# Two column halves: splitting every convolution matmul of an ODE-net kernel into two 64-column matmuls

## The reference

```
def _L0_conv_ref(x):                       # a DCT over rows and columns
    y = jnp.einsum('kh,bchw->bckw', Dh, x)
    y = jnp.einsum('lw,bckw->bckl', Dw, y)
    return y

def odefunc(t, y):                         # the second layer
    h = jax.nn.relu(_group_norm(y, gn1_w, gn1_b))
    h = _concat_conv(t, h, conv1_w, conv1_b)      # 3 x 3, 33 -> 32 channels, one of them is t
    h = jax.nn.relu(_group_norm(h, gn2_w, gn2_b))
    h = _concat_conv(t, h, conv2_w, conv2_b)
    return _group_norm(h, gn3_w, gn3_b)

def step(y, t):
    return (y + dt * odefunc(t, y), None)  # NUM_STEPS = 6, dt = 1/6
```

## Time and profile before

| what | us |
|---|---|
| median of 2 runs (3930.53 to 3938.78) | 3934.66 |
| span of the profiled execution | 3928.6 |
| PE busy (91% of the span) | 3592.0 |
| PEld busy (52%) | 2039.1 |
| DVE busy (85%) | 3342.3 |
| ACT busy (53%) | 2079.6 |
| POOL busy (24%) | 929.9 |

### The profile page before, as it was taken

How to read it: one execution, slowest core, us unless ns; L and a number is a source line. 1 busy time by engine, 2 the same in 40 slices (tenths; PEclk the granted TensorE clock), 3 DMA queues, 4 the chain that set the end, 5 groups by cost and what they waited for, 6 DMA issues and landing times.

```text
span 3928.6 us, 70526 instructions
## 1 busy us (share of the span) xinstructions
PE 3592.0 (91%) x21844; PEld 2039.1 (52%) x21844; DVE 3342.3 (85%) x7423; ACT 2079.6 (53%) x3169; POOL 929.9 (24%) x1589
## 2 busy tenths in 40 slices
PE   3699999999999999999999999999999999999995
PEld 3455554555555555555555555555555555554553
DVE  7688888888888888888888888888888888888885
ACT  0455565555655556555565545655555555655553
POOL 4022212222122221222212231123211322111211
PEclk7899999999999999999999999999999999999998
DMA  3300033113032130311312113311133112231013
GB/s 79 74 17 16 22 45 84 41 60 70 11 84 62 61 58 10 94 63 41 58 42 83 41 41 58 76 49 41 41 58 84 41 41 62 37 83 49 25 41 99
DMA packets 366284, 210.26 MB, mean 54 GB/s; under 512 B 351104, under 2 KB 351472, under 8 KB 364016
## 3 DMA queue, kind: packets, MB, share of 16 engines
q1 hardware_dynamic: 366064, 207.66, 21.2%
HBM read 104.88 MB, written 77.07 MB: 46 GB/s over the span
## 4 chain that ended last, share of the span: by engine, by line
issue 39%; PE 34%; DVE 14%; POOL 10%; ACT 2%; POOLq 1%; DMA 1%; DVEq 0%; SPq 0%; ACTq 0%
PE cps L1246 30%; POOL xn L516 3%; POOL small L479 3%; DVE hb L973 2%; POOL m L513 2%; POOL xn L521 2%; PE xps L1320 2%; DVE hb L976 2%; ACT z L620 2%; DVE bnt L889 1%; POOL hb L496 1%; DVE bnt L896 1%; DVE small L951 1%; DVE bn L1000 1%; DVE ha L976 1%
## 5 line engine op out<-in xcount | busy, mean ns | idle before, releaser
L1246 PE MATMUL cps<-ha,w 128*128 128x399 f16 (+1 forms) x9216 | 1737.6, 342 | 69.7 <-DVE ha L976 64.5
L1246 PE MATMUL cps<-hb,w 128*128 128x448 f16 x8064 | 1645.0, 360 | 0.0
L608 ACT ACTIVATE z<-cps,bias_now 128x448 f32<-128x448 f32 (+2 forms) x1440 | 875.8, 610 | 1128.3 <-PE cps L1246 1100.9
L1246 PEld LDWEIGHTS cps<-ha,w 128*128 128x128 f16 x9216 | 861.0, 99 | 693.6 <-ACT z L608 61.1
L1246 PEld LDWEIGHTS cps<-hb,w 128*128 128x128 f16 x8064 | 748.9, 100 | 678.8 <-issue 41.5
L479 POOL TENSOR_TENSOR small<-small,half 128x1 f32<-128x1 f32 x304 | 190.3, 626 | 2135.6 <-DVE small L942 2133.8
L496 POOL MEMSET hb<- 64x28 f16 (+2 forms) x1152 | 320.5, 278 | 784.6 <-DVE hb L976 666.2
L889 DVE BATCH_NORM_STATS2 bnt<-z 128x6 f32<-128x448 f32 x672 | 413.1, 621 | 94.7 <-ACT z L608 94.7
L620 ACT ACTIVATE z<-z,small 128x798 f32<-128x798 f32 (+1 forms) x384 | 405.8, 1057 | 120.5 <-DVE small L951 120.5
L982 DVE SCALAR_TENSOR_TENSOR y<-z,small,y 128x784 f32<-128x784 f32 x384 | 457.4, 1245 | 6.7
L896 DVE BATCH_NORM_STATS2 bnt<-z 128x6 f32<-128x385 f32 (+1 forms) x768 | 411.4, 546 | 56.9 <-ACT z L608 50.4
(11 more groups left out here) (135 smaller groups left out, 2352.4 us busy)
## 6 DMA issues: line engine op xcount, KB each, us to landing
xa<-x_dram SPq DMA_DIRECT2D x64, 392.0 KB, 7.9
y<-xa SPq DMA_DIRECT2D x16, 1568.0 KB, 7.7
y_dram<-y SPq DMA_DIRECT2D x64, 392.0 KB, 7.1
xs<-in_x_dram SPq DMA_DIRECT2D x31, 784.0 KB, 8.7
x_dram<-x1s SPq DMA_DIRECT2D x30, 784.0 KB, 5.3
fin<-y_dram SPq DMA_DIRECT2D x30, 784.0 KB, 7.8
fin<-x_dram SPq DMA_DIRECT2D x28, 784.0 KB, 8.3
out_dram<-fin SPq DMA_DIRECT2D x28, 784.0 KB, 3.3
```

The lines of the kernel that those rows point to most:

```text
L608: nc.scalar.activation(z[slot][:, r0 * width:(r0 + r) * width], cps[i % BANKS][:, 0:r * width], ACT.Identity, bias=bias_now[:, conv:conv + ...
L1246: return pe.matmul(ps, w[:, tap, wl, :], h[:, hl, r0 + a:r0 + a + r, b:b + width], start=(n == 0), stop=(n == len(products) - 1))
```

## The change

Each of the twelve products of a tile is issued as two matmuls: one with weight columns 0 to 63 that writes PSUM partitions 0 to 63, and one with weight columns 64 to 127 that writes partitions 64 to 127. Both have the same moving operand, all 128 rows of it and all its 399 to 456 elements. In the built program a matmul of before occupies an array tile of 128 x 128; the two that replace it occupy tiles of 128 x 64 at column positions 0 and 64. The rim, statistics and DCT matmuls keep the full-width tile. `tile_done` is raised by the second half of the last product. Nothing is changed on the other engines.

```
-                def product(n):
+                def product(n, half):
                     tap, wl, hl = products[n]
                     a, b = tap // 2, tap % 2
-                    return pe.matmul(ps, w[:, tap, wl, :], h[:, hl, r0 + a:r0 + a + r, b:b + width],
+                    m = slice(64 * half, 64 * half + 64)
+                    return pe.matmul(ps[m], w[:, tap, wl, m], h[:, hl, r0 + a:r0 + a + r, b:b + width],
                                      start=(n == 0), stop=(n == len(products) - 1))
 
                 for m in range(len(products) - 1):
 
                     if (k, m) in between:
                         between[k, m]()
-                    product(m)
+                    for half in range(2):
+                        product(m, half)
...
-                product(len(products) - 1).then_inc(tile_done, 1)
+                product(len(products) - 1, 0)
+                product(len(products) - 1, 1).then_inc(tile_done, 1)
```

## The result

The changed kernel takes 4341.36 us (median of 2 runs, 4327.78 to 4354.94) where the kernel before takes 3934.66: 1.1035 times as long, 95% interval 1.0949 to 1.1121. The forecast was 4,500 with a range of 3,840 to 4,950, and slower. The profiled execution's span is 4326.0 us, 397.4 more than that of before.

A forecast was written before the change was run, and what follows sets the result against it. PE, busy 91% of the span, was taken to set the pace. Span 3,928.6 + 461 (tile width changes) + 195 (other groups) + 80 (loads) - 160 (swallowed waits) = 4,505, given as 4,500 us, range 3,840 to 4,950.

The forecast's parts named there:

- Streams: Two halves of a product stream at once: no change taken; upper bound, one following the other, 3,145 us more.
- Changes of width: At 2,880 tile changes around rims the hidden tail shows, 0.17 us behind a product, 0.15 behind a rim: 461 us.
- Weight loads: Half-width loads at 0.056 us each, hidden within runs of products, one uncovered per tile at the rim: 80 us.
- The other groups: Full-width statistics, means and DCT groups, 590 in all, each add a pair of width changes at 0.33 us: 195 us.
- what is swallowed: PE's waits for ACT and DVE shrink as its tiles lengthen: 160 of 226 us taken off.
- Issue: Four instructions a product on PE in place of two cost nothing, as two pairs start within 0.18 us.
- Its lower end for the tails: Low end of the likeliest case: a third of a tail, 0.05 us a change, half of that swallowed: 4,150 us.
- The signs it named: Expected in the changed profile: halves together in 2.30 us, longer distances around rims, shorter PE waits, middle clock at 0.98.
- Nearly free changes: Rival: width changes cost almost nothing; halves' stagger and uncovered loads remain, up to 187 us; about 3,980 us, chance 0.28.
- one stream after the other: Rival: the two halves of each product follow each other, 3,145 us more; 6,850 to 7,100 us, chance 0.12.
- bare loads: Rival: half-width weight loads don't go under a running matmul, 1,935 us more; about 5,700 us, chance 0.07.
- faster: Rival: fully independent halves each cover the other's 0.005 us gap, 86 us saved; 3,843 us, chance 0.03.

The follow-up runs named there:

- halves-apart run: Changed kernel with each tile's eleven lower-half products issued first, then the eleven upper ones, then rim and twelfth product: 6210.81 us in a single run.
- all halves: Unrolled changed kernel with the rim, statistics, mean and DCT matmuls also issued as two halves: 3931.26 us, 0.9988 of before.

## Why the prediction was right, and where its sizes were not

**The bound** held: PE sets the pace in both, and DVE, at 78%, did not become the limit.

**Streams** were taken at the lower of two bounds 3,145 us apart, on the ground that the halves share no column and no output. That was the choice on which all rested, and it was right: pairs start 0.003 us apart, and ten second halves a tile taken away give 79 us, of which the loop's wait explains 40. The halves-apart run adds what the argument left out: side by side needs near neighbours in the program.

**Changes of width** were the right term, shown by four runs that move it and little else (the rims in both kernels, all halves, the sixth product whole), and mis-sized. The prediction took the whole hidden tail, 0.17 us ahead of a rim and 0.15 behind; measured are 0.099 and 0.087, 267 us for the tiles where it had 461. The next matmul starts at 0.288 us, ahead of the modelled end of the record at 0.36. The upper bound was the wrong end to take as a value; about 0.6 of it was paid. The Trainium skill, "TensorEngine Tiling (Array Packing)", section "Key Properties", says that a change of tiling mode drains the engine, and gives no price. The trace agrees in so far as each change costs about 0.1 us and the kernel in which nothing changes mode is back at the time of before; a wait to the modelled end of the record is not seen.

What the prediction did not see is that the weight load is held as well. Timeline of PE, then PEld, at a rim of the changed kernel, to be read beside the earlier trace rows, where the rim's load starts at 2003.95 and the rim at 2004.13:

```profile
2033.14 0.19 PE L1264 MATMUL cps<-rim_i,rim_w 128*128 128x14 f16 x1
...
2033.14 0.10 PEld L1264 LDWEIGHTS cps<-rim_i,rim_w 128*128 x1 [0.33 <-issue]
```

By medians the rim's load starts 0.186 us ahead of the rim in the kernel before and in the one with halved rims, and 0.004 us ahead in the changed kernel. So behind a change the load no longer lies under the matmul ahead. How the 0.1 us divides between the array's tail and this bare load no run separates.

**Weight loads.** The term of 80 us for bare loads measured 28. Its price came from a misread row: the DCT's 0.098 us was put down to its loads, and the run with halved DCTs shows that it is the stream. Nor are two half-width float16 loads 0.11 us: in the changed kernel those behind a rim start 0.003 us apart, and the next pair of loads follows after 0.028. In the kernel with halved rims the loads at the rims are nearly free (from a rim to the product 0.028 us as before, from a closing product to the next 0.175 where before had 0.171), so the 80 us of its expectation were not paid. It came out only 44 us under it, since PE's way to the groups took 44 us longer again.

**The other groups, and what is swallowed.** The prediction had 195 us for changes of width at statistics and DCT groups and took 160 off. The waits of PE for other engines fell from 291 to 192 us, 99. All in all the groups and the plain products come to 17.8 - 20.2 = -2 us. In the changed kernel the groups' changes added 87 us within and behind them, and 69 us came back on the way to them, where PE, delayed at the rims, waited less. So the delay at the rims seems to pay for them: in the kernel with halved rims, without that delay, they cost 90 us (4021.1 to 3931.26).

**What was missing** is the loop's jump: the wait of 75.0 us where there had been 5.1, and with it 101 us at the first tiles of conv 0. "Issue: four instructions a product cost nothing" looked at the pace of instructions within a run, where it holds, and not at their number in the loop's body. The sum of 576 us had its tile terms too high by 242 (541 against 299), the groups less what is swallowed too high by 37 (35 against -2), and lacked the 101: 576 - 242 - 37 + 101 = 398. The errors partly cancel, and that is luck: without the loop's jump, which nothing in the prediction foresaw, the terms named would have missed by 279 us.

**The range.** Its lower end for the tails, 4,150, does not follow from its working: 4,060 changes at 0.05 us are 203 us, with half of that swallowed about 4,030, and about 4,110 with the 80 us for loads. The measured time lies above all three.

**The signs it named.** 24 half-width matmuls were to span about 2.30 us: 2.44, of which 0.10 is the way to the rim. The way to the rim was to be over 0.30 (0.288), that behind it about 0.18 or more (0.12): above before, below the forecast. Of the waits for L729 and L976, the first halved and the second stayed. The granted clock in the middle was 0.99.

**The rivals.** Nearly free changes, one stream after the other, bare loads and faster each miss by more than the prediction does, and each has a run against it: halved rims in the kernel before (207 us for changes alone), the taken-away halves, the flat pace of pairs within a tile, and the kernel all in halves, where independent halves gain 0.1% at most.

## What to carry to other kernels

Splitting a matmul into column halves is free when the halves stand next to each other and their neighbours have the same width; every passage between half and full width cost about 0.1 us here, in either direction, so a kernel should be in one width throughout, down to its smallest matmuls. Count a change's passages before its streams: 2,880 of them made 267 us, 7% of the time before, and 17,280 extra matmuls none by themselves. When a loop's body grows, look at the instruction queue and at the waits on nothing behind the jumps too.

## What the runs showed of the hardware

- Two 64-column matmuls with one moving operand stream side by side at the pace of one 128-column matmul: 448 columns every 0.19 us at a granted clock of 1.00 (2.4 GHz), pairs 0.003 us apart.
- Going from half to full width or back adds about 0.09 to 0.11 us between starts, less than the 0.17 us by which a record outlasts its stream, and the weight load behind the change starts with its matmul (0.004 us ahead) where it had started 0.186 us ahead.
- A half-width matmul can start ahead of three waiting ones for the other half (18 places for 22 streams), so starts do not strictly follow the program.
- A float32 record of 112 moving columns keeps 0.096 to 0.098 us whether its load has 112, 64 or 48 columns (a group of eight records is four matmuls of the program).
- A loop body can outgrow what is kept: fetched instructions rose from 1.61 to 5.72 MB with a wait of about 2.8 us at a turn (75.0 over 27), and with 30 matmuls and loads fewer in a step they were 2.51 MB and the waits at the inner loop's turns were gone. Behind 10 of the 27 waits the granted clock was 0.50, and products of 456 columns took 0.38 us.
